# y3 of the second half of the tokens: stored once and split in the last stage instead of before the store

## What is computed

```python
x = x + _L2_ffn_ref(_L2_cond_ref(...), ...)              # base product plus two LoRA experts per token
# layer 3
out = jnp.einsum('boi,bih->boh', agg_w, x) + agg_b[:, :, None]       # cond: mixes the 64 channels of a batch, gives y3
logits = jnp.einsum('bsh,he->bse', y3, gate_w)                       # ffn
h = jax.nn.relu(jnp.einsum('bsh,hi->bsi', y3, up_w)) ** 2
shared_out = jnp.einsum('bsi,ih->bsh', h, down_w)
moe_out = expert_out * jnp.sum(top2(logits), axis=-1, keepdims=True)
x = x + _layernorm(shared_out + routed_out, ln_gamma, ln_beta)
```

## Time and profile before

| | |
|---|---|
| median of 3 runs | 1654.09 us (1651.56 to 1657.61) |
| the profiled execution | 1651.25 us |
| its span, first to last instruction | 1649.5 us |
| TensorE busy | 1576.2 us, 96% |
| VectorE / ScalarE / GpSimd busy | 823.7 / 506.4 / 315.2 us |
| moved by DMA | 238.57 MB |
| mean granted TensorE clock | 0.988 |

### The profile page before, as it was taken

How to read it: one execution, slowest core, us unless ns; L and a number is a source line. 1 busy time by engine, 2 the same in 40 slices (tenths; PEclk the granted TensorE clock), 3 DMA queues, 4 the chain that set the end, 5 groups by cost and what they waited for, 6 DMA issues and landing times.

```text
span 1649.5 us, 20620 instructions
## 1 busy us (share of the span) xinstructions
PE 1576.2 (96%) x7752; PEld 1284.4 (78%) x7752; DVE 823.7 (50%) x1336; ACT 506.4 (31%) x761; POOL 315.2 (19%) x262
## 2 busy tenths in 40 slices
PE   7899879999998889999999999999999999999996
PEld 5688558889976558877888888887788888888875
DVE  4567578895374537772333333332723333333336
ACT  3344325333265521223222222212232222222122
POOL 1000022234155530122211111112112101111110
PEclk9999999999999999999999999999999999999999
DMA  9765635556774757894531111114925311111115
GB/s 308 224 197 166 139 97 182 167 186 212 243 241 126 288 194 291 301 321 155 111 92 51 51 51 51 51 52 140 319 77 100 83 49 51 51 51 51 52 41 177
DMA packets 117241, 238.57 MB, mean 145 GB/s; under 512 B 22503, under 2 KB 61551, under 8 KB 115778
## 3 DMA queue, kind: packets, MB, share of 16 engines
q1 hardware_dynamic: 80890, 154.75, 28.2%
q0 software_dynamic: 23008, 68.24, 13.8%
q10 hardware_dynamic: 13264, 14.52, 3.2%
HBM read 164.51 MB, written 89.19 MB: 154 GB/s over the span
## 4 chain that ended last, share of the span: by engine, by line
PE 77%; DVE 4%; POOL 2%; issue 2%; DMA 1%; ACT 1%; SPq 0%; ACTq 0%; DVEq 0%; POOLq 0%
PE pu L1956 27%; PE pd L1956 26%; PE l_po L1956 7%; PE pf L1956 6%; POOL scratch_pairs L1464 2%; PE l_ea L1313 2%; PE pw L648 2%; PE pw L647 2%; PE l_ea L1889 1%; PE l_po L1889 1%; PE pg L1085 1%; PE l_ea L1904 1%; PE l_tr L1904 1%; DMA scratch_g<-latent_out 1%; DMA scratch_expert_out<-expert_out,pair_ids 0%
## 5 line engine op out<-in xcount | busy, mean ns | idle before, releaser
L1956 PE MATMUL pd<-down_hi,hid_hi 128*128 128x512 f32 x640 | 249.1, 389 | 2.9 <-issue 2.9
L1956 PE MATMUL pu<-y_hi,up_hi 128*128 128x512 f32 x640 | 250.5, 391 | 0.6 <-issue 0.6
L1956 PE MATMUL pu<-y_lo,up_hi 128*128 128x512 f32 x640 | 250.3, 391 | 0.0
L1956 PE MATMUL pu<-y_hi,up_lo 128*128 128x512 f32 x640 | 250.3, 391 | 0.0
L1956 PE MATMUL pd<-down_hi,hid_lo 128*128 128x512 f32 x640 | 249.0, 389 | 0.0
L1956 PE MATMUL pd<-down_lo,hid_hi 128*128 128x512 f32 x640 | 249.0, 389 | 0.0
L2257 DVE TENSOR_TENSOR hid_lo<-hidden,hid_hi 128x512 fp32r<-128x512 f32 x64 | 44.3, 692 | 391.5 <-ACT hid_hi L2165 391.5
L2087 POOL TENSOR_TENSOR down_lo<-raw,down_hi 128x1024 fp32r<-128x1024 f32 x40 | 100.3, 2508 | 681.2 <-ACT down_hi L2102 681.2
L2159 ACT ACTIVATE hidden<-pu 128x512 f32<-128x512 f32 x64 | 38.3, 598 | 470.0 <-PE pu L1956 470.0
L2196 DVE TENSOR_TENSOR acc<-pd,acc 128x512 f32<-128x512 f32 x224 | 143.6, 686 | 54.7 <-PE pd L1956 51.4
L1956 PEld LDWEIGHTS pd<-down_hi,hid_hi 128*128 128x128 f32 x640 | 120.1, 188 | 28.8 <-issue 3.7
(11 more groups left out here) (324 smaller groups left out, 2494.5 us busy)
## 6 DMA issues: line engine op xcount, KB each, us to landing
l_x<-scratch_x SPq DMA_DIRECT2D x32, 512.0 KB, 6.5
delta<-scratch_expert_out SPq DMA_DIRECT2D x32, 512.0 KB, 6.8
raw<-in_up SPq DMA_DIRECT2D x32, 512.0 KB, 3.6
raw<-in_down SPq DMA_DIRECT2D x32, 512.0 KB, 4.3
X<-scratch_x SPq DMA_DIRECT2D x248, 64.0 KB, 2.6
y1T<-in_x SPq DMA_DIRECT2D x16, 512.0 KB, 9.8
scratch_x<-y1T SPq DMA_DIRECT2D x16, 512.0 KB, 3.0
scratch_x<-l_x SPq DMA_DIRECT2D x16, 512.0 KB, 5.5
```

What stands on the lines that cost most here:

```text
L1956: mm = pe.matmul(out, lhs[a], rhs[b], start=first and n == 0, stop=last and n == len(pairs) - 1)
```

## The change

y3 of tiles 8 to 15 is no longer split in layer 2. Each tile is stored once, unsplit, through four buffers in turn (n % 4, n = t - 8), to one array in HBM. `load_y` reads it back once per block, into `y_raw`, which lies where `y[1]` lies. It is split there during the ending step of the first half: eight pieces of 128x1024 (two feature chunks by 512 tokens), four per block. ScalarE casts the four of block 0 ahead of `norm`, and two of block 1 ahead of each of its tiles 1 and 2. VectorE subtracts the four of block 0 at the head of the step, ahead of the addition of tile 0, and one of block 1 behind each of tiles 2 to 5. TensorE's `y_there` waits for the four low parts of a block instead of the loads.

```diff
-    names["y3"] = [at(f"l2_y3_{i}", address, [P, D]) for i, address in enumerate((slot(7), LAST, slot(9), slot(11)))]
-    names["y3h"] = [at(f"l2_y3h_{i}", slot(n), [P, D], F32R) for i, n in enumerate((1, 13, 10, 12))]
+    names["y3"] = [at(f"l2_y3_{i}", address, [P, D]) for i, address in enumerate((slot(7), LAST, slot(1), slot(13)))]
...
@@ phase_l2, gpsimd
-                    pool.wait_ge(y3_hi, t + 1)
-                    pool.dma_start(SC["y3"][0][:, :, n * P:(n + 1) * P],
-                                   y3h[y3_slot(t)][:].bitcast(F32).rearrange("p (k j) -> p k j", k=KC)).then_inc(y3_stored[t % 2], 16)
-                    pool.wait_ge(y3_lo, n + 1)
-                    pool.dma_start(SC["y3"][1][:, :, n * P:(n + 1) * P],
-                                   y3[y3_slot(t)][:].rearrange("p (k j) -> p k j", k=KC)).then_inc(y3_stored[t % 2], 16)
+                    pool.wait_ge(y3_made, 2 * (t + 1))
+                    pool.dma_start(SC["y3"][:, :, n * P:(n + 1) * P],
+                                   y3[n % 4][:].rearrange("p (k j) -> p k j", k=KC)).then_inc(y3_stored[n % 4], 16)
...
@@ phase_l2, scalar
             for t in mixed_tiles(s):
-                act.wait_ge(y3_made, 2 * (t + 1))
                 if t < NT // 2:
-                    if t == NT // 2 - 1:
-                        act.wait_ge(x3b_stored[1], 16 * 2)
-                        act.wait_ge(x3b_stored[2], 16 * 2)
+                    act.wait_ge(y3_made, 2 * (t + 1))
                     cols = slice(t * P, (t + 1) * P)
                     act.copy(y[0][:, :, cols], y_raw[:, :, cols]).then_inc(y3_hi, 1)
-                else:
-                    if NT // 2 + 2 <= t < NT - 2:
-                        act.wait_ge(y3_stored[t % 2], 32 * ((t - NT // 2) // 2))
-                    act.copy(y3h[y3_slot(t)][:], y3[y3_slot(t)][:]).then_inc(y3_hi, 1)
                 if t + 2 < NT:
                     mats_in(t + 2)
...
@@ phase_l2, vector, y3_out
-            if NT // 2 + 2 <= t < NT - 2:
-                dve.wait_ge(y3_stored[t % 2], 32 * ((t - NT // 2) // 2))
-            elif t == NT // 2:
-                dve.wait_ge(x3b_stored[3], 16 * 2)
+            n = t - NT // 2
+            if n >= 4:
+                dve.wait_ge(y3_stored[n % 4], 16)
+            elif n in (0, 2, 3):
+                old = {0: 7, 2: 5, 3: 6}[n]
+                dve.wait_ge(x3b_stored[old % 4], 16 * (old // 4 + 1))
...
@@ phase_l2, vector
             for t in mixed_tiles(s):
-                y3_low(t)
+                if t < NT // 2:
+                    y3_low(t)
...
@@ phase_l3
+    YP = KC // 2
+
+    def y_piece(n, c):
+
+        return slice(2 * c, 2 * c + 2), slice(n * HALF, (n + 1) * HALF)
...
@@ phase_l3, gpsimd, load_y
             for n in range(NB):
                 pool.wait_ge(up_mm, Q * (g + 1) - NB + 1 + n)
-                for part in range(2):
-                    cols = slice(n * HALF, (n + 1) * HALF)
-                    pool.dma_start(y[part][:, :, cols], SC["y3"][part][:, :, cols]).then_inc(y_loaded[n], 16)
+                cols = slice(n * HALF, (n + 1) * HALF)
+                pool.dma_start(y_raw[:, :, cols], SC["y3"][:, :, cols]).then_inc(y_loaded[n], 16)
...
@@ phase_l3, scalar
+        def y_high(n, c):
+            k, cols = y_piece(n, c)
+            act.wait_ge(y_loaded[n], 16)
+            act.copy(y[0][:, k, cols], y_raw[:, k, cols]).then_inc(y_hi, 1)
+
-        def norm(half):
+        def norm(half, again):
 
             for T in range(HT * half, HT * (half + 1)):
+                if again and T % HT in (1, 2):
+                    for c in range(2):
+                        y_high(1, 2 * (T % HT - 1) + c)
                 act.wait_ge(centred, T + 1)
...
                 act.wait_ge(h_lo, Q * g + 2)
-                norm(half - 1)
+                if front:
+                    for c in range(YP):
+                        y_high(0, c)
+                norm(half - 1, front)
...
@@ phase_l3, vector
+        def y_low(n, c):
+            k, cols = y_piece(n, c)
+            dve.wait_ge(y_hi, YP * n + c + 1)
+            dve.tensor_tensor(y[1][:, k, cols], y_raw[:, k, cols], y[0][:, k, cols].bitcast(F32), ALU.subtract).then_inc(y_lo[n], 1)
+
...
             if end:
+                if front:
+                    for c in range(YP):
+                        y_low(0, c)
                 for t in range(HT):
                     T = HT * (half - 1) + t
...
                     centre(T)
+                    if front and 2 <= t < 2 + YP:
+                        y_low(1, t - 2)
                 finish(T)
...
@@ phase_l3, tensor, y_there
             if half:
-                pe.wait_ge(y_loaded[n], 32)
+                pe.wait_ge(y_lo[n], YP)
```

More of the change, by code:

```diff
@@ L1242, in phase_l2 @@
         "B B_raw y2s y2 war blank lg below every pos expert_of ids G Gd res brow brow_raw bias_tmp val taken pick").split()]
-    half_tmp, rT, eo, x3, d, mats, bias3, y3, y3h, y, y_raw, ea, tr, po = [buf[n] for n in (
-        "half_tmp rT eo x3 d mats bias3 y3 y3h y y_raw ea tr po").split()]
+    half_tmp, rT, eo, x3, d, mats, bias3, y3, y, y_raw, ea, tr, po = [buf[n] for n in (
+        "half_tmp rT eo x3 d mats bias3 y3 y y_raw ea tr po").split()]
     ge, key, lg2, ex, posf, steps, count, steps_int, pair_int, compare, prod = [buf[n] for n in (
@@ L1255, in phase_l2 @@
     R1A, R1B, R2A = 15, 23, 36
-    mats_loaded, bias3_loaded, d_loaded, y3_stored, y_ready, y_loaded = [s_.slot_sems(n) for n in (
-        "mats3_loaded bias3_loaded delta_loaded y3_stored y_ready l2_y_loaded").split()]
+    mats_loaded, bias3_loaded, d_loaded, y_ready, y_loaded = [s_.slot_sems(n) for n in (
+        "mats3_loaded bias3_loaded delta_loaded y_ready l2_y_loaded").split()]
+    y3_stored = s_.slot_sems("y3_stored", 4)
     x3_loaded, x3b_stored, eo_stored = s_.slot_sems("l2_x3_loaded", 4), s_.slot_sems("x3b_stored", 4), s_.slot_sems("expert_stored", 4)
@@ L1264, in phase_l2 @@
         "l2_bias_lo ones_cut gate_hi gate_lo pair_ids route_step exp_done rank_mm pairs_stored l2_B_top l2_B_half l2_B_rest")
-    (row_ids, twice, tr_mm, r_hi, r_lo, eo_mm, eo_act, eo_dve, mats_zeroed, d_first, x3_made, y_mm, y3_made, y3_hi, y3_lo) = s_.sems(
+    (row_ids, twice, tr_mm, r_hi, r_lo, eo_mm, eo_act, eo_dve, mats_zeroed, d_first, x3_made, y_mm, y3_made, y3_hi) = s_.sems(
         "row_ids pair_twice pair_turned rT_hi rT_lo expert_mm expert_out_act expert_out_dve mats3_zeroed delta_first x3_made y3_mm y3_made "
-        "y3_hi y3_lo")
+        "y3_hi")
     def chunk(c):
@@ L1751, in y3_out @@
                 else:
-                    out = y3[y3_slot(t)][:, chunk(h)].rearrange("p (c k) -> p c k", c=4)
+                    out = y3[n % 4][:, chunk(h)].rearrange("p (c k) -> p c k", c=4)
                 dve.tensor_tensor(out, py[t % 2][h][:].rearrange("p (c k) -> p c k", c=4),
@@ L1980, in phase_l3 @@
         "up_hi up_lo down_hi down_lo up_mm relu squared hid_hi hid_lo down_mm added")
-    g_mm, gT_made, g_turned, g_out, topped, g_summed = s_.sems(
-        "gate_mm gateT_made gate_turned gate_out gate_topped gate_summed")
+    g_mm, gT_made, g_turned, g_out, topped, g_summed, y_hi = s_.sems(
+        "gate_mm gateT_made gate_turned gate_out gate_topped gate_summed y3_again_hi")
+    y_lo = s_.slot_sems("y3_again_lo")
+    YP = KC // 2
+    def y_piece(n, c):
+        return slice(2 * c, 2 * c + 2), slice(n * HALF, (n + 1) * HALF)
     gamma_loaded, eps_set, centred, ssq_made, rooted, inverted, weighed, out_made = s_.sems(
@@ L1997, in mixed_stored @@
         for sem in y3_stored:
-            eng.wait_ge(sem, 32 * NT // 4)
+            eng.wait_ge(sem, 32)
     def first_up_hi(act, i):
@@ L2222, in gate_top @@
             if half == 0:
-                dve.wait_ge(y3_stored[1], 32 * NT // 4)
+                dve.wait_ge(y3_stored[1], 32)
             dve.tensor_copy(logits[:], pd[0][1][:, 0:HT * EG]).then_inc(g_out, 1)
@@ L2380, in build @@
     SC["mats"] = [nc.dram_tensor(f"scratch_mats{i}", (BATCH, CH * CH), F32).ap() for i in range(2)]
-    SC["y3"] = [nc.dram_tensor(f"scratch_y3_{part}", (P, KC, NT // 2 * P), F32).ap() for part in ("hi", "lo")]
+    SC["y3"] = nc.dram_tensor("scratch_y3", (P, KC, NT // 2 * P), F32).ap()
     SC["pairs"] = nc.dram_tensor("scratch_pairs", ((NEXP + 1) * P, RW), F32).ap()
```

10 lines of the change are left out of this document (2 added, 8 removed).

## The result

| | before | after |
|---|---|---|
| median of 8 runs each | 1653.49 us (1650.53 to 1657.61) | 1664.36 us (1659.42 to 1668.34) |
| the profiled execution, its span | 1651.25, 1649.5 us | 1662.0, 1660.3 us |
| moved by DMA | 238.57 MB | 230.18 MB |
| VectorE / ScalarE / GpSimd busy | 823.7 / 506.4 / 315.2 us | 819.8 / 505.8 / 303.7 us |

What follows compares the result with a forecast made beforehand. TensorE, busy 96%, was taken to bound the kernel. Seam -1.1, stall +8.2, VectorE lateness +0.9 and clock +2.2 sum to +10.2 us: 1664.3 us against a median of 1654.09, range 1657 to 1669 (forecast's own bounds 1659 to 1667.5).

Steps and rivals of the forecast that it cites:

- What bounds the kernel: Whole kernel: TensorE is busy 96%, so only stretches where it idles or runs at its lower clock matter.
- the removed work at 0: Layer 2's mix stage: casts, subtractions and stores taken away lie beside a full TensorE, so they gain 0 us.
- The seam, -1.1: Layer 2 to layer 3: earlier deltas gain 0.35 us, an earlier up_lo 0.75 us, together -1.1 us.
- The landing, 13.6: Head of the first half's ending step: the first y load lands 13.6 us after its issue, at 1154.3.
- The stall, 8.2: Ending step: first addition 11.9 us later, less 3.7 us slack, so TensorE waits 8.2 us at the third tile.
- VectorE late at tile 6, 0.9: End of the ending step: block 1's pieces make VectorE late, delaying the gate block 0.9 us, bounds 0.4 and 1.5.
- The clock, 2.2: Behind the stall: TensorE partly runs at 1.2 GHz, costing 2.2 us, bounds 0 and 3.4.
- The sum, +10.2: Whole kernel: seam, stall, VectorE lateness and clock together make it 10.2 us slower, 1664.3 us against the median.
- (a): Rival, ending step: y load lands near 1150, stall about halved to 4.2 us; +4.0 us, 1658.1 us; chance 0.12.
- (b): Rival, ending step: y loaded by 1146.1, no stall, not slower; 1653.9 us, or 1652.2 without a dip; chance 0.10.
- (c): Rival, ending step: engines lock into one chain, TensorE waits again at tiles 3 to 7; 1668.0 us; chance 0.08.

Runs made afterwards that it cites:

- e7: Kernel before, with the y3 casts and subtractions of tiles 14 and 15 moved behind layer 3's first weights: 1651.36 us against 1652.81, ratio 0.9984.
- e5: Changed kernel, with ScalarE's two first x3b loads (1 MB) issued behind its four casts: 1658.81 us against 1652.81 for the kernel before, ratio 1.0029.
- e3: Kernel before, plus one VectorE wait for y's first-block loads ahead of the ending step's first addition: 1666.09 us against 1654.15, ratio 1.007.
- e8: As e6, with VectorE's first-block subtractions behind tiles 1 to 4 instead of 2 to 5: 1653.04 us against 1652.92, ratio 0.9988.
- e2: Kernel before, with only layer 3's half of the change (stored high part loaded, split in the ending step): 1662.8 us against 1654.15, ratio 1.0051.
- after's second profile: Changed kernel, unaltered, run and profiled again on another experiment's chip: 1661.85 us against 1652.81 for the kernel before, ratio 1.0055.
- e4: Changed kernel, pieces spread over later tiles, GpSimd subtracting block 1's four: 1663.1 us against 1654.15 for the kernel before, ratio 1.0049.
- e6: As e4 without GpSimd's pieces: VectorE subtracts block 1 after its last normalization, first upward product between gate blocks; 1652.53 us against 1652.81, ratio 0.9997.

## Why the prediction was right

**What bounds the kernel, and the removed work at 0.** Right. VectorE fell from 14.5 to 10.5 and ScalarE from 4.0 to 1.5 us in the window from 700 to 720, and no long wait of TensorE had hung on it. At 0 it was a little too low: 0.1 to 0.6 us come back between the mixes of tiles 8 and 14, which the prediction did not count.

**The seam, -1.1.** Right in its mechanism, slightly small. From the mix of tile 14 to the ending step: 409.58 less 1.6 for the dip, against 406.54, so -1.4 us. e7 shows 0.8 of it as VectorE's and ScalarE's queues; the remaining 0.6 fits the earlier deltas (7.0 instead of 4.5 us ahead), and that part was not tried by itself.

**The landing, 13.6.** Right: 13.8 and 13.8 in two profiles. The argument, transfers of one queue finish in order and what stands behind doesn't matter, held: two loads fewer behind it changed nothing (13.6 to 13.8). What stands beside it on another queue does matter, 2.5 us for the 1 MB of x3b (e5). The landing also shares its time with 1 MB of weights that the prediction did not count: in the 13.8 us of after the DMA engines move 335 GB/s, 4.6 MB and not 3.1, and from 1145 to 1155 they move 377 GB/s. The 3.8 us that the Trainium skill's 358 GB/s would have taken off ("DMA: Bandwidth & Descriptors", Specifications) were not there because of these bytes; by that rate and 1 us to the first byte an estimate for 4.6 MB is 13.9 us, close to the trace's 13.8, though its 377 GB/s in the middle is above the limit.

One reading of the prediction is wrong, that the load can't be issued earlier because the old y is in use. GpSimd's queue in after, ahead of the load:

```profile
1137.22 2.49 POOL L2077 TENSOR_TENSOR down_lo<-raw,down_hi 128x1024 fp32r<-128x1024 f32 x1 [8.39 <-ACT down_hi L2092]
1139.65 1.87 POOL L2058 DMA_DIRECT2D y_raw<-scratch_y  x2
```

TensorE's last product that reads block 0 is done at about 1134.6 (24 products of the next quarter, 0.227 us each, follow it up to 1139.9); the load stood behind `down_lo`, and from 1134.6 to 1139.6 the DMA engines moved 2 GB/s. Issued 5 us sooner, the load would, by e5's 11.3 us, land at about 1146.0, the chain of 5.7 us behind it would reach the first addition at about 1151.7, and a stall of about 0.6 us would be left instead of 8. That is an estimate; no run tried it.

**The stall, 8.2.** Right: 8.13 and 8.15 in the two profiles, by the mechanism named: e3 makes it with a wait alone, e5 shortens it by what the landing shortens.

**VectorE late at tile 6, 0.9.** Right mechanism (e8), mis-sized: 0.27. The piece costs VectorE 1.13 us from start to start (1172.25 to 1173.38), not 1.23, and the instruction ahead of it 1.20 instead of its duration of 1.28, so a tile takes 5.51 us, 0.07 over TensorE's, not 0.2 to 0.3.

**The clock, 2.2.** Right in size in the stall: 1.5 in one profile of after, 2.3 in the other, 2.6 and 2.9 in e2 and e3 (each the ending step's excess over 45.72 less its waits), and in these last three the lower level lasted 10.2 instead of 6.8 us. What I did not see is that the dips elsewhere move too: after has one more behind the gate block, +1.6, and none near 765 us, -1.6 against before; after's second profile has neither change behind the gate block. The dips move in code that is equal; beside them the stretch up to the mix of tile 14 differs by up to 8 us from profile to profile. The lower level takes 24 to 41 us of it, but not in step with its length (24 in the profiles of 730.4 and 733.0 us), and the cause is open.

**The sum, +10.2.** In terms: -1.4 + 8.14 + 0.27 + 1.5 to 2.3 = +8.5 to +9.3, and a dip more or less. The whole ruler, dips included, gives +8.5 and +7.7 us for the two profiles, and the gain ahead of tile 14 takes a little more off. The runs gave +10.9 and, the second time, +9.1 us, by their intervals at least 8.3 and 6.1. So the ruler's sums lie at the low side, and some 2 us of the difference between the medians are in no term; the code that is equal up to the mix of tile 8 scatters by more than that. That the median came out within 0.1 us of the forecast is more than the terms are good for, and luck: the term of VectorE was 0.6 too high, and the interval of the runs reaches 2.6 us to either side. The prediction's own bounds are not quite its sum either: 1659 is all lower ends together, which it says are not met at once, and all upper ends together give 1667.2, not 1667.5.

**The rivals.** (a) fell at the landing, (b) at 1146.1, where the load would have had to be there; (c) did not occur: behind the third tile TensorE has no wait until the gate block.

## What to carry to other kernels

A step that is moved into a later stage takes its data's arrival with it: before work is put at the head of an engine's queue, ask when its input lands and who waits for the instructions behind it on that engine, not how long it takes (one bare wait cost e3 as much as eight casts and eight subtractions cost the change). The same work set between the later additions and behind the last one cost the ending step nothing (45.69 against 45.72 us, e8). And ask what holds the load's issue: here a subtraction ahead of it on GpSimd's queue, not the buffer. Where equal code differs by several us between executions, compare stretches between fixed instructions, not spans.

## What the runs showed of the hardware

**A GpSimd subtraction and a VectorE instruction on two SBUF inputs hold each other up.** In e4 the four VectorE instructions that overlap a GpSimd subtraction take 3.2 to 3.9 us instead of 1.2 to 1.3. Where VectorE was first, in the kernel before, it kept its 1.23 us and GpSimd took 3.27 instead of 2.5:

```profile
765.76 1.23 DVE L2179 TENSOR_TENSOR up_lo<-raw,up_hi 128x1024 fp32r<-128x1024 f32 x1
765.95 3.27 POOL L2087 TENSOR_TENSOR down_lo<-raw,down_hi 128x1024 fp32r<-128x1024 f32 x1 [11.49 <-ACT down_hi L2102]
```

Being first is not all of it: the one of 3.88 us in e4 is recorded as started 0.4 us ahead of GpSimd's. Additions of VectorE with one input in PSUM are not slowed; in the kernel before, four of them beside a GpSimd subtraction take 2.69 us, 0.67 from start to start (all 224 instructions of this line take 0.68 to 0.69 each):

```profile
1339.51 2.49 POOL L2087 TENSOR_TENSOR down_lo<-raw,down_hi 128x1024 fp32r<-128x1024 f32 x1 [19.11 <-ACT down_hi L2102]
1339.65 2.69 DVE L2196 TENSOR_TENSOR acc<-pd,acc 128x512 f32<-128x512 f32 x4
```

The Trainium skill states the contention ("GPSIMD Engine Reference", Key points: GpSimd shares its SBUF interfaces with VectorE, with contention for VectorE instructions in a 2-port mode or with two SBUF inputs); these rows agree, and I had not weighed it in e4.

**The time at the lower clock is not fixed by the stall.** A stall of about 8 us brought 6.8 or 10.2 us at 1.2 GHz, part of it inside the stall, for 1.5 to 2.9 us lost; the stall of 5.5 us in e5 brought 6.8 us, for 2.1 lost. The second half's gate blocks are followed by a dip of 3.4 us in nine profiles and by none in e6 and e7, and e7 has there the code of the kernel before.
